# Softmax weights of a decoder layer: the second copy goes from VectorE to ScalarE from the second batch on, a sixth buffer of turned weights, and new orders on all engines

## The reference, cut to what matters

```python
Q = (X @ Wq.T + bq).reshape(B, S, 16, 32) * scale          # K the same, V without scale
scores = jnp.where(causal, jnp.einsum('bqhd,bkhd->bhqk', Q, K), -jnp.inf)
attn = jax.nn.softmax(scores, axis=-1)
x = _layernorm(x + jnp.einsum('bhqk,bkhd->bqhd', attn, V).reshape(B, S, D) @ Wo.T + bo)
energy = (ctx @ xWq.T + bq) @ (ctx @ xWk.T + bk).T          # per batch, 512 x 512
x = _layernorm(x + x @ softmax(energy).T)
xq = quantise(rms_norm(x))                                   # 8-bit steps, one step per row
p = silu(xq @ sign(W_g).T) * (xq @ sign(W_u).T)              # 2048 hidden
x = _layernorm(x + p @ sign(W_d).T)
```

## Time and profile before

| | |
|---|---|
| median of 3 runs | 628.76 us (626.74 to 629.14) |
| the profiled execution, its own time | 626.21 us |
| its span, first to last instruction | 624.2 us |
| mean granted TensorE clock, as a share of full speed | 0.964 |
| busy, share of the span: TensorE, VectorE, GpSimd, ScalarE | 89%, 79%, 65%, 63% |

### The profile page before, as it was taken

One profiled execution on the slowest core, in us unless ns is written; L12 is line 12 of the kernel. 1 busy time (PEld: TensorE's weight loads), 2 busy tenths in 40 slices (PEclk: granted clock), 3 DMA queues, 4 the chain that ended last, 5 costly groups with the idle time before them and its releaser, 6 DMA issues. The chain is left out here.

```text
span 624.2 us, 14611 instructions
## 1 busy us (share of the span) xinstructions
PE 552.5 (89%) x5532; PEld 352.1 (56%) x5532; DVE 494.7 (79%) x1264; ACT 396.3 (63%) x741; POOL 408.1 (65%) x421
## 2 busy tenths in 40 slices
PE   5996595669999999898989999989989998999996
PEld 4464362347645656465656566567555565575572
DVE  5778654576899878979896877887998889878675
ACT  5899776375578776567567654465776876444151
POOL 1366735578387878768675666765677889846443
PEclk9998598769999999999999999999999999999999
DMA  9899999987366959898852719485295799852000
GB/s 319 318 248 208 241 217 234 242 144 128 69 103 117 193 122 186 162 162 136 145 96 43 149 41 180 77 153 127 50 156 107 121 204 154 144 93 59 18 35 34
DMA packets 241381, 89.55 MB, mean 143 GB/s; under 512 B 227872, under 2 KB 232480, under 8 KB 239776
## 3 DMA queue, kind: packets, MB, share of 16 engines
q1 hardware_dynamic: 240768, 88.11, 70.0%
q10 hardware_dynamic: 544, 0.52, 0.2%
HBM read 27.79 MB, written 4.19 MB: 51 GB/s over the span
## 5 line engine op out<-in xcount | busy, mean ns | idle before, releaser
L1203 POOL TENSOR_TENSOR ph<-p,ph 128x768 f16<-128x768 f32 (+1 forms) x96 | 174.1, 1818 | 69.5 <-ACT ph L793 43.9
L853 ACT ACTIVATE p<-ps_b,tops 128x128 f32<-128x128 f32 (+3 forms) x256 | 119.9, 535 | 51.4 <-DVE tops L1022 27.5
L1022 DVE CUSTOM_DVE_ANT_0 ps_b<-ps_b,future 128x128 f32<-128x128 f32 (+3 forms) x256 | 117.9, 518 | 17.5 <-PE ps_b L682 17.3
L760 PE MATMUL ps_b<-xqT,sg 128*128 128x256 f16 x1024 | 119.7, 273 | 4.5 <-DVE o L1043 1.0
L775 PE MATMUL ps_b<-sd,hp 128*128 128x512 fp8e4 x512 | 118.3, 379 | 2.0 <-DVE gt L1126 1.5
L760 PEld LDWEIGHTS ps_b<-xqT,sg 128*128 128x128 fp8e4 x1024 | 97.2, 98 | 26.4 <-ACT p L853 3.8
L1199 POOL TENSOR_TENSOR hp<-gt,hp 128x512 f16<-128x512 f32 x64 | 76.1, 1196 | 47.6 <-ACT hp L793 47.6
L626 PE MATMUL ps_b<-xhl,wh 128*128 128x256 f16 x480 | 84.9, 276 | 8.0 <-DVE o L1043 4.8
L775 PEld LDWEIGHTS ps_b<-sd,hp 128*128 128x128 f16 x512 | 47.9, 98 | 56.8 <-issue 1.7
L626 PE MATMUL ps_b<-xhl,wl 128*128 128x256 f16 x240 | 66.3, 276 | 0.0
L932 ACT ACTIVATE gt<-gt 128x512 f32<-128x512 f32 x64 | 40.0, 630 | 36.2 <-DVE gt L1121 36.1
(11 more groups left out here) (112 smaller groups left out, 910.9 us busy)
## 6 DMA issues: line engine op xcount, KB each, us to landing
hp<-in_sgT_dram SPq DMA_DIRECT2D x6, 1024.0 KB, 6.8
gt<-in_sgT_dram SPq DMA_DIRECT2D x6, 1024.0 KB, 7.7
rows<-in_x_dram SPq DMA_DIRECT2D x8, 512.0 KB, 4.6
out_dram<-rows SPq DMA_DIRECT2D x16, 256.0 KB, 2.2
xin<-in_xT_dram SPq DMA_DIRECT2D x14, 256.0 KB, 3.6
e<-in_ctxT_dram SPq DMA_DIRECT2D x4, 512.0 KB, 4.5
pt<-ph SPq DMA_TRANSPOSE x96, 4.3
hp<-in_wT_dram SPq DMA_DIRECT2D x4, 256.0 KB, 4.8
```

Of the source, the lines that this page charges most:

```text
L760: ins = pe.matmul(ps[:, a * HALF:(a + 1) * HALF], sg[:, ("gg", "uu").index(name), c, ht * P:(ht + 1) * P], xqT[:, c, :], start=c == 0, sto ...
L853: ins = act.activation(p32[:, n % P32_SLOTS, to:to + keys], ps[:, col:col + keys], ACT.Exp, scale=-1.0, bias=tops[:, s % 2, g, j, qt % 2:q ...
L1022: ins = dve.tensor_tensor_reduce(scores, scores, future[:, S - width:S], EXP_SCALE, 3e38, ALU.add, ALU.min, tops[:, s % 2, g, j, qt % 2:qt ...
L1203: pool.tensor_tensor(out_, in_, hi, ALU.subtract).then_inc(signal, 1)
```

## The change

Four edits are made.

First, from pair 24 on (the second batch), ScalarE makes the high half of both pairs: its list gains 36 entries `hi....1` and VectorE's loses them. GpSimd then waits for ScalarE's signal alone. Second, the 12 copies that stay on VectorE, all in the first batch, are issued as a maximum of the weights with themselves in place of a copy. Third, `pt` has 6 buffers in place of 5; part of the room comes from the buffer set aside for DMA descriptors of GpSimd's queue, which this kernel does not use. Fourth, all five lists are new, with new banks. The tasks in them are otherwise the same.

```diff
-P32_SLOTS, PH_SLOTS, PT_SLOTS, HP_SLOTS = 3, 3, 5, 6
+P32_SLOTS, PH_SLOTS, PT_SLOTS, HP_SLOTS = 3, 3, 6, 6
+SHARED = 24
...
@@ p_high on VectorE
-                dve.tensor_copy(ph[:, n % PH_SLOTS, 0:width], p32[:, n % P32_SLOTS, 0:width]).then_inc(p_hi[1].sem, 1)
+                weights = p32[:, n % P32_SLOTS, 0:width]
+                dve.tensor_tensor(ph[:, n % PH_SLOTS, 0:width], weights, weights, ALU.max).then_inc(p_hi[1].sem, 1)
...
@@ p_low on GpSimd
-                wait(pool, p_hi[pair], 0, n // 2 + 1)
+                if n < SHARED:
+                    wait(pool, p_hi[pair], 0, n // 2 + 1)
+                else:
+                    wait(pool, p_hi[0], 0, n - SHARED // 2 + 1)
...
-    nc = bacc.Bacc("TRN2", target_bir_lowering=False, num_devices=1, dynamic_dma_scratch_size=4096)
+    nc = bacc.Bacc("TRN2", target_bir_lowering=False, num_devices=1, dynamic_dma_scratch_size=1024)
```

Of the lists, the start of TensorE's, and the part of it around the feed-forward block of the second batch's first half (`ib2`, `gg1.0`):

```diff
-qp qk0.0.0@7 qk0.0.1@6 qk0.0.3@4 qk0.0.2@5 va0.0.0@3 va0.0.1@2 bv@3 cp0.1@5 cp0.0@2 mx0.0.0.0@3,4,6,7 qk0.1.0@1
-en0.2@5 en0.1@6 en0.0@7 va0.1.0@4 va0.1.1@1 mx0.0.1.0@6,7,2,3 qk0.1.1@4 pv0.0.0.0@5 pv0.0.0.1@5 qk0.1.2@1
-mx0.0.2.0@7,4,6,0 qk0.1.3@3 pv0.0.0.2@5 pv0.0.0.3@5 en0.3@4 mx0.0.3.0@1,6,7,2 pv0.0.1.0@5 pv0.0.1.1@5
+qp qk0.0.0@7 qk0.0.1@6 qk0.0.3@4 qk0.0.2@5 va0.0.0@3 va0.0.1@2 mx0.0.0.0@3,6,7,1 bv@5 cp0.1@6 cp0.0@5
+mx0.0.1.0@7,2,3,4 mx0.0.2.0@7,5,1,0 en0.2@6 en0.1@2 en0.0@3 en0.3@4 pv0.0.0.0@5 pv0.0.0.1@5 qk0.1.0@3 pv0.0.0.2@5
...
-pv2.0.3.3@7 qk2.1.3@5 mx2.1.0.1@2,3,4,6 ib2@1 gg1.0.0@7 uu1.0.0@1 cp2.0@2 cp2.1@3 uu1.0.2@7 uu1.0.1@2 uu1.0.3@4
...
+pv1.1.2.2@4 pv1.1.2.3@4 qk2.0.1@1 mx2.0.0.0@4,5,3,6 qk2.0.3@2 va2.0.1@4 ib2@6 va2.0.0@3 mx2.0.1.0@2,6,7,1 pv1.1.3.0@5
+pv1.1.3.1@5 gg1.0.0@0 gg1.0.1@2 uu1.0.0@6 pv1.1.3.2@5 pv1.1.3.3@5 uu1.0.2@7 uu1.0.1@0 uu1.0.3@2 uu1.0.5@3 pv2.0.0.0@4
```

And a part of ScalarE's, in the third batch:

```diff
-ex2.1.2.0 ex2.1.2.1 ex2.1.2.2 hi2.1.2.0.0 ex2.1.2.3 qk3.0.0 n12.0.0 ex2.1.2.4 ex2.1.2.5 ex2.1.2.6 hi2.1.2.1.0
+ex2.1.2.0 ex2.1.2.1 qk3.0.0 ex2.1.2.2 ex2.1.2.3 ga1.1.5 hi2.1.2.0.0 ga1.1.6 hi2.1.2.0.1 hh1.1.5 qk3.0.1 ex2.1.2.4
```

More of the change, by code:

```diff
@@ L89 @@
[L89 to L93, removed]
@@ L130 @@
[L130 to L134, removed]
@@ new lines @@
+mx0.0.1.0@7,2,3,4 mx0.0.2.0@7,5,1,0 en0.2@6 en0.1@2 en0.0@3 en0.3@4 pv0.0.0.0@5 pv0.0.0.1@5 qk0.1.0@3 pv0.0.0.2@5
+pv0.0.0.3@5 pv0.0.1.0@0 pv0.0.1.1@0 va0.1.0@2 va0.1.1@3 mx0.0.3.0@2,5,1,7 pv0.0.1.2@0 pv0.0.1.3@0 qk0.1.1@6
+mx0.1.0.0@1,3,5,2 pv0.0.2.0@7 pv0.0.2.1@7 qk0.1.2@4 qk0.1.3@1 mx0.1.0.1@4,5,6,0 pv0.0.2.2@7 pv0.0.2.3@7
+mx0.1.1.0@5,4,2,3 pv0.0.3.0@7 pv0.0.3.1@7 pv0.0.3.2@7 pv0.0.3.3@7 va1.0.0@0 va1.0.1@7 mx0.1.1.1@2,4,5,6 qk1.0.0@3
+qk1.0.1@1 qk1.0.2@4 qk1.0.3@3 mx0.1.2.0@3,4,1,2 op0.0.0@5 op0.0.1@6 pv0.1.0.0@5 pv0.1.0.1@5 pv0.1.0.2@5 pv0.1.0.3@5
@@ new lines @@
+pv2.0.0.1@4 pv2.0.0.2@4 pv2.0.0.3@4 gg1.0.2@5 gg1.0.3@0 pv2.0.1.0@6 pv2.0.1.1@6 gg1.0.5@1 gg1.0.4@4 uu1.0.4@5
+dn1.0.1.0@7 pv2.0.1.2@6 pv2.0.1.3@6 dn1.0.0.0@0 qk2.1.0@2 qk2.1.1@5 mx2.0.2.0@2,3,1,4 qk2.1.2@6 qk2.1.3@3
+mx2.0.3.0@4,5,1,2 dn1.0.1.1@7 op1.1.0@6 pv2.0.2.0@3 pv2.0.2.1@3 mx2.1.0.0@2,1,5,4 op1.1.1@6 pv2.0.2.2@3 pv2.0.2.3@3
+uu1.0.6@1 uu1.0.7@5 pv2.0.3.0@6 pv2.0.3.1@6 gg1.0.7@2 gg1.0.6@4 pv2.0.3.2@6 pv2.0.3.3@6 va2.1.0@3 xm1.1.0@6
+mx2.1.0.1@3,5,1,2 xm1.1.1@4 va2.1.1@3 mx2.1.1.0@2,4,1,5 dn1.0.0.1@0 dn1.0.0.2@0 dn1.0.1.2@7 cp2.0@4 cp2.1@1
@@ new lines @@
+pv2.1.0.0@2 pv2.1.0.1@2 mx2.1.1.1@4,5,3,6 dn1.0.0.3@0 en2.0@4 en2.1@3 pv2.1.0.2@2 pv2.1.0.3@2 en2.2@6 en2.3@0
+gg1.1.2@5 ib3@4 dn1.0.1.3@7 gg1.1.0@4 gg1.1.3@2 gg1.1.1@7 uu1.1.0@3 uu1.1.2@1 uu1.1.1@4 pv2.1.1.0@3 pv2.1.1.1@3
+uu1.1.3@7 uu1.1.5@0 pv2.1.1.2@3 pv2.1.1.3@3 uu1.1.4@4 uu1.1.6@6 gg1.1.4@5 qk3.0.1@3 op2.0.0@7 op2.0.1@5
+mx2.1.2.0@7,4,1,2 qk3.0.0@5 gg1.1.5@7 gg1.1.6@4 gg1.1.7@1 dn1.1.1.0@5 xm2.0.1@7 mx2.1.2.1@6,4,0,2 xm2.0.0@3
+dn1.1.0.0@0 mx2.1.3.0@3,2,4,6 uu1.1.7@7 dn1.1.0.1@0 dn1.1.0.2@0 mx2.1.3.1@4,2,3,1 dn1.1.1.1@5 pv2.1.2.0@6 pv2.1.2.1@6
@@ new lines @@
+qk0.0.2 qk0.0.3 va0.0.0 cs0.0 cs0.1 sg0 va0.0.1 ex0.0.0.0 ex0.0.0.1 sg1 ex0.0.0.2 ex0.0.0.3 hi0.0.0.0.0 cp0.0 cp0.1
+ex0.0.1.0 xs0.1.0 xs0.1.1 ex0.0.1.1 ex0.0.1.2 hi0.0.1.0.0 ex0.0.1.3 ex0.0.2.0 ex0.0.2.1 sg2 ex0.0.2.2 en0.0 en0.1
+ex0.0.2.3 hi0.0.2.0.0 ez0.0 sg3 qk0.1.0 ov0.0.0 ez0.1 ta0.0 ta0.1 va0.1.0 sg4 en0.2 va0.1.1 en0.3 ex0.0.3.0 ex0.0.3.1
+ex0.0.3.2 ex0.0.3.3 qk0.1.1 ov0.0.1 hi0.0.3.0.0 ez0.2 ex0.1.0.0 ex0.1.0.1 ez0.3 qk0.1.2 ex0.1.0.2 ex0.1.0.3 ta0.2
+qk0.1.3 ta0.3 ov0.0.2 ex0.1.0.4 ex0.1.0.5 hi0.1.0.0.0 xs1.0.0 xs1.0.1 sg5 ex0.1.0.6 ex0.1.0.7 sg6 ov0.0.3 hi0.1.0.1.0
@@ new lines @@
+zn0.1.0 ex1.1.3.2 hi1.1.3.0.0 ex1.1.3.3 zn0.1.1 hi1.1.3.0.1 ex1.1.3.4 ov1.1.2 ex1.1.3.5 ex1.1.3.6 ex1.1.3.7
+hi1.1.3.1.0 qk2.0.1 qk2.0.2 n11.0.1 ex2.0.0.0 ex2.0.0.1 hi1.1.3.1.1 ex2.0.0.2 ex2.0.0.3 qk2.0.3 hi2.0.0.0.0 ib2
+hi2.0.0.0.1 ex2.0.1.0 ex2.0.1.1 ex2.0.1.2 hi2.0.1.0.0 ga1.0.0 ga1.0.1 ex2.0.1.3 va2.0.0 va2.0.1 ov1.1.3 hh1.0.0
+hi2.0.1.0.1 xs2.1.0 xs2.1.1 to1.1.0 hh1.0.1 to1.1.1 ov2.0.0 ga1.0.2 hh1.0.2 ga1.0.3 ov2.0.1 hh1.0.3 ga1.0.4 ga1.0.5
+hh1.0.4 qk2.1.0 hh1.0.5 qk2.1.1 ex2.0.2.0 ex2.0.2.1 ex2.0.2.2 ex2.0.2.3 hi2.0.2.0.0 hi2.0.2.0.1 qk2.1.2 qk2.1.3
@@ new lines @@
+mx0.1.0.1 mx0.1.0.2 mx0.1.0.3 ov0.0.1 qk0.1.1 qk0.1.2 mx0.1.0.4 mx0.1.0.5 mx0.1.0.6 mx0.1.0.7 qk0.1.3 ov0.0.2
+mx0.1.1.0 mx0.1.1.1 mx0.1.1.2 mx0.1.1.3 hi0.1.0.0.1 ov0.0.3 mx0.1.1.4 mx0.1.1.5 hi0.1.0.1.1 mx0.1.1.6 mx0.1.1.7
+qk1.0.0 qk1.0.1 qk1.0.2 qk1.0.3 mx0.1.2.0 hi0.1.1.0.1 mx0.1.2.1 mx0.1.2.2 mx0.1.2.3 op0.0.0 os0.0.0 op0.0.1 os0.0.1
+mx0.1.2.4 mx0.1.2.5 mx0.1.2.6 hi0.1.1.1.1 mx0.1.2.7 ov0.1.0 hi0.1.2.0.1 mx0.1.3.0 mx0.1.3.1 mx0.1.3.2 mx0.1.3.3
+xm0.0.0 xm0.0.1 n10.0.0 n20.0.0 n10.0.1 n20.0.1 hi0.1.2.1.1 ov0.1.1 mx0.1.3.4 mx0.1.3.5 mx0.1.3.6 mx0.1.3.7
@@ L286 @@
+dn3.1.0 dn3.1.1
 """
```

330 lines of the change are left out of this document (156 added, 174 removed).

## The result

The changed kernel takes 609.12 us (median of 4 runs, 606.53 to 610.69) where the kernel before took 628.15 beside it: a ratio of 0.9695, 95% interval 0.9655 to 0.9734. A second measurement of the same kernel gave 0.9696 (0.9670 to 0.9721). The profiled execution took 609.27 us of its own time, with a span of 607.3 us.

The account below looks back on a forecast made before the run. The middle was taken as bound by TensorE's own work with 25.6 us of gaps, the first batch partly by transfers; -6.6 + 1.4 - 2.5 = -7.7 us gave 621.0 us, 8-in-10 range 611 to 632.

Parts of the forecast that it names:

- VectorE without 36 copies: Middle, 137 to 600 us: taking 36 copies off VectorE was to close half of TensorE's 12.6 us gaps, -6.3 us.
- ScalarE with 36 copies: Middle: ScalarE's 5.7 us of gaps were to grow with its load, +0.7 us; the copies' own time counted as hidden.
- sixth buffer: Middle: no direct gain, but an order in which TensorE may use turned weights later, counted at -1 us.
- 12 maxima: First batch: up to +5.4 us of VectorE time if maxima wait for GpSimd; a quarter on the path, +1.4 us.
- start of the lists: First batch: scores issued earlier let low halves, transposes and transfers start earlier; between 0 and 4.6 us, taken as -2.5.
- I add nothing for it: Middle: early `ib2` and `gg1.0` spread VectorE's gate work, a means to the half of 12.6 us; 0 added.
- VectorE's account, half of 12.6 us: Middle: TensorE's gaps ended by VectorE, 12.6 us; VectorE's free time rises by half, so half goes, -6.3 us.
- I count the two as even: Middle: second low half up to 0.86 to 1.05 us later, against first low half no longer queuing behind VectorE's copy.
- ScalarE's queue delays the exponentials: Rival, chance 0.12: in attention-only stretches two copies in a row delay the second pair; +16.6 us less 7.7, 637 us.
- whatever the compute engines do: First batch, 60 to 80 and 100 to 120 us: transfers leave no room, with DMA shares over 1.
- The rival in which the gaps of the first batch close: Rival, chance 0.10: new order keeps TensorE supplied and its clock high there; -13 us on top of -6.6, 609 us.
- each held the other: At 255 us: a VectorE copy and GpSimd's low halves were read as delaying each other; copy ended at 258.09.

## Why the prediction was right and wrong

The kernel went faster by 19.1 us and not by 7.7. The middle was named as the place and held the gain. What failed is the account of it. In the table, "by" names the comparison; times are differences of ratios except where a trace is named.

| step | predicted, us | shown, us | by |
|---|---|---|---|
| VectorE without 36 copies | -6.3 | -9.8 | nobody copies, old lists |
| ScalarE with 36 copies | +0.7 | +0.1 in the new lists, +20.4 in the old | with and without |
| new lists in the middle | 0 | -9.4, with the three rows below in it; -10.5 in the middle of the traces | nobody copies, old against new |
| sixth buffer | -1 | up to -4.3, in the new lists; 0 in the old | five buffers |
| 12 maxima | +1.4 | +1.4, not told from 0; some +2 to +3 in the traces | as copies |
| start of the lists | -2.5 | about -3 without the maxima | `ib0` at 130.5 us before, 127.5 with copies |

**The step that failed: "I add nothing for it".** The prediction took the new lists of the middle only as the means by which half of VectorE's gaps could be closed. They were worth 9.4 us beyond all that lifting the 36 copies gives, and they are also what made the copies free on ScalarE: the same copies cost 20.4 us in the old lists. The traces put the gain in the middle. Here is the start of the first and of the last feed-forward block's transposes, and the time between, one trace each; the two rows of old lists with VectorE copying differ by 2.3 us, which shows how far one trace can be trusted:

| | first, us | last, us | between, us |
|---|---|---|---|
| before | 130.5 | 587.8 | 457.3 |
| before with six buffers | 130.9 | 590.5 | 459.6 |
| old lists, nobody copies | 131.0 | 581.4 | 450.4 |
| old lists, ScalarE copies | 129.8 | 596.6 | 466.8 |
| new lists, nobody copies | 128.8 | 568.7 | 439.9 |
| changed kernel | 130.8 | 570.7 | 439.9 |
| changed kernel with load put back | 130.6 | 593.8 | 463.2 |

Of the 17.4 us that the middle lost, 6.9 came with the lifted copies and 10.5 with the new lists; ScalarE's copies then add nothing. So the effects don't add up as my sum had it. Moving the copies without new lists is a loss of 10.6 us (1.0169), and new lists without the moved load lose all their gain, at the places where I put it back (1.0096). Which of the lists' changes gives the gain was not isolated, and the new PSUM banks are part of them. The early `ib2` is the most visible one.

**VectorE's account, half of 12.6 us.** The size was fair: 9.8 us by the ratios (give or take 1.9) and 6.9 in the trace, where 6.3 was forecast. But it was read from the wrong column. The sums of TensorE's waits in the middle, by what ended them last, made from all groups of each run as for the earlier trace rows:

| | VectorE | ScalarE | DMA |
|---|---|---|---|
| before, 137 to 600 us | 12.6 | 5.7 | 5.1 |
| old lists, nobody copies, 137 to 593 us | 8.7 | 1.0 | 6.5 |
| changed kernel, 137 to 583 us | 3.8 | 2.2 | 2.3 |
| changed kernel with 37 us of load put back, 137 to 606 us | 17.7 | 9.5 | 0 |

The run with nobody copying was traced in its slowest execution (620.16 us), so its row is of a gain of 6 us and not of 9.8. Lifting load from VectorE alone took more from ScalarE's column (4.7 us) than from its own (3.9), and putting load back filled both. ScalarE's own waits suggest why. In the changed kernel its longest (from 137 to 580 us, total, times, longest) are for VectorE:

```profile
ACT gt L935 <- DVE gt L1125: 24.1, 21, 3.7
ACT hp L796 <- DVE gt L1138: 17.7, 16, 2.2
...
ACT p L856 <- DVE tops L1025: 12.1, 10, 3.3
```

The last of these is an exponential that waits for VectorE's row maxima. Where TensorE then waits for that exponential, the wait stands under ScalarE's name; how much of the 4.7 us came in this way was not counted.

**"I count the two as even" and +0.7 for ScalarE.** Right in the sum, but not for the reason that I gave. ScalarE's free time hides the copies only in the new lists; in the old ones, with as much of it free, they cost 20.4 us. The rival "ScalarE's queue delays the exponentials" named the right place for the old lists, and its price came out near (+16.6 us for half of the pairs, 20.4 measured), but partly by luck: it was made of the copies' own 0.92 us each, and what the trace shows is their waits for a `ph` buffer, which the prediction doesn't mention. I gave the rival against a kernel with other lists, and didn't read them for it.

**The sixth buffer.** Nothing in the old lists, as said; in the new ones -1 was probably too little (4.3 us, give or take 2.6). There it decides whether a transpose of weights holds other transposes in SyncE's queue.

**The first batch.** The first transpose came before 37 us, as said:

```profile
36.07 7.06 SPq L571 DMA_TRANSPOSE pt<-ph  x3
```

yet `ib0` starts at 130.8 us, no earlier than before. With the 12 as copies it starts at 127.5, about the 2.5 us that I gave the new start; so the start of the lists seems to earn what was forecast, and the maxima to spend it. The reading "whatever the compute engines do", for the stretches with DMA shares over 1, was wrong: TensorE did 3.5 us more between 60 and 80 us at a share of 1.05. The rival in which the gaps of the first batch close gave 609 us, the time that was measured, but its mechanism didn't happen, as 38.5 of 39.9 us of gaps are still there; the number is a coincidence.

**The maxima.** The groups gave 1156 and 1838 ns for 768 and 1024 columns:

```profile
L1034 DVE TENSOR_TENSOR ph<-p 128x768 f16<-128x768 f32 x8 | 9.2, 1156 | 2.0 <-ACT p L856 2.0
L1034 DVE TENSOR_TENSOR ph<-p 128x1024 f16<-128x1024 f32 x4 | 7.4, 1838 | 0.0
```

That is 16.6 us for the 12. As copies in the same lists they took 8 x 0.751 + 4 x 1.043 = 10.2 us, so +6.4 us of VectorE time, where I had +5.4 for the upper bound. On the path I had +1.4, which is also the difference of the ratios (0.0023 x 628), but that is inside the uncertainty, and `ib0` suggests more. One reading of the rows was also too strong: in the earlier trace rows GpSimd's next low half waits for that copy's signal, so "each held the other" is shown there only for the copy that waited for GpSimd. VectorE's busy time was to be 463 us and ScalarE's 430; they are 469.6 and 421.5. The copies and maxima account for what was forecast, so other instructions changed by some +6 and -8 us, which I didn't follow.

**The last 24 us**: nothing, as said.

## What to carry to other kernels

Where every engine runs a fixed list, price a moved operation by where it stands in the new list: what it waits for (here a free buffer, up to 4.3 us) and what stands behind it, and give the new order a term of its own in the sum. That the cost follows from what stands behind is my reading; that it depends on the lists is measured (20.4 us in one pair, 0.1 in the other). The gaps put down to an engine by its last release are not its account, as the engines named beside it wait for it too. Before crediting a change to one of its parts, run it with the work left out on both orders: here that split 19.1 us into 9.8 for the load and 9.4 for the order. The split holds for that way round; the two work together, as putting the load back in the new order cost 25 us.

## What the runs showed of the hardware

A maximum with both inputs in SBUF and GpSimd's low halves delay each other. Timeline of VectorE, and of GpSimd around it, changed kernel:

```profile
72.39 2.14 DVE L1034 TENSOR_TENSOR ph<-p 128x1024 f16<-128x1024 f32 x1
```
```profile
71.18 2.27 POOL L1207 TENSOR_TENSOR xhl<-xin,xhl 128x512 f16<-128x512 f32 x2
...
74.61 2.13 POOL L1207 TENSOR_TENSOR ph<-p,ph 128x1024 f16<-128x1024 f32 x1 [1.16 <-DVE ph L1034]
```

GpSimd ended at 73.45 us and the maximum at 74.53, 1.08 us later. GpSimd's next low half needs the maximum's result, so its 1.16 us of waiting are no sign of the other direction. That shows at the first of the 12. Timelines of VectorE and GpSimd with maxima, then the same place in the run with reductions:

```profile
32.70 1.85 DVE L1034 TENSOR_TENSOR ph<-p 128x768 f16<-128x768 f32 x1 [1.54 <-ACT p L856]
```
```profile
31.24 2.50 POOL L1243 TENSOR_TENSOR rows<-rows,bo 128x512 f32<-128x512 f32 x2 [3.59 <-DVE bo L1000]
33.69 3.96 POOL L1207 TENSOR_TENSOR ph<-p,ph 128x768 f16<-128x768 f32 x2
```
```profile
34.10 0.95 DVE L1034 TENSOR_REDUCE ph<-p 128x768 f16<-128x768 f32 x1 [1.53 <-ACT p L856]
```
```profile
32.65 2.50 POOL L1243 TENSOR_TENSOR rows<-rows,bo 128x512 f32<-128x512 f32 x2 [3.59 <-DVE bo L1000]
35.10 3.24 POOL L1207 TENSOR_TENSOR ph<-p,ph 128x768 f16<-128x768 f32 x2
```

Both started while GpSimd was still busy with `rows`. The maximum took 1.85 us, where the shortest took 0.948, and GpSimd's two low halves, due at 33.69 while it ran, took 3.96 us. The reduction took its 0.95 us all the same, and the two low halves 3.24. A reduction over an axis of length one gives the same values and took 0.94 to 0.95 us for 768 columns and 1.21 to 1.22 for 1024 in all 12 cases. A copy is faster alone (0.550) but took up to 1.453. The Trainium skill, "SBUF — State Buffer", section "Who interferes with whom", says that an operation with two SBUF inputs contends with GpSimd's reads and a reduction never does; the trace agrees (1.85 us against 0.95 beside the same work of GpSimd).

After the gap of 7.67 us in the run with five buffers, TensorE's granted clock was 0.76 in a 20 us window in which the changed kernel ran at full clock. The timeline shows the same pair of matmuls at two rates:

```profile
504.68 1.03 PE L629 MATMUL ps_b<-wh,oT 128*128 128x512 f16 x2 [7.67 <-DMA oT<-ohl]
...
509.72 0.60 PE L629 MATMUL ps_b<-wh,oT 128*128 128x512 f16 x2
```

Each pair with the matmul behind it took about 1.27 us up to 509 us and 0.65 from 509.72 on, so the stall cost, by my estimate from these rows, some 2.4 us beyond its length in this stretch.
